# Two cross-attention layers: key stacks loaded a unit ahead in layer 0, slot by slot in layer 1

## The reference

```
layer 0:  q = x Wq + 2 x Aq Bq          32 heads
          k, v likewise from ctx          8 heads, each shared by 4 query heads
          x = x + (softmax(q k' / 4) v) Wo'    (Wo' with its low-rank part)
layer 1:  q = x Wq + bq, k = ctx Wk + bk, v = ctx Wv + bv    32 heads each
          masked keys get -inf before the softmax
          x = layernorm(x + (softmax(q k' / 4) v) Wo + bo) * g + b
```

## Time and profile before

| | |
|---|---|
| median of the runs | 1661.51 us (1660.65 to 1664.09) |
| the profiled execution's own time | 1668.17 us |
| its span, first to last instruction | 1666.3 us |
| mean granted TensorE clock | 0.967 of 2.4 GHz |
| PE, VectorE, ScalarE, GpSimd busy | 95%, 73%, 60%, 11% of the span |
| DMA | 168.22 MB, 101 GB/s over the span |

### The profile page before, as it was taken

One profiled execution on the slowest core, in us unless ns is written; L12 is line 12 of the kernel. 1 busy time (PEld: TensorE's weight loads), 2 busy tenths in 40 slices (PEclk: granted clock), 3 DMA queues, 4 the chain that ended last, 5 costly groups with the idle time before them and its releaser, 6 DMA issues.

```text
span 1666.3 us, 42831 instructions
## 1 busy us (share of the span) xinstructions
PE 1581.1 (95%) x17828; PEld 1133.7 (68%) x17828; DVE 1216.4 (73%) x2669; ACT 1005.8 (60%) x1855; POOL 177.6 (11%) x274
## 2 busy tenths in 40 slices
PE   6899999999999999899989999999989999999997
PEld 3657666676666765655667777776767677777763
DVE  2667778677777777678867777588777778778782
ACT  0146666566666666576656666656656666666665
POOL 2000221001221011121211110000000001000000
PEclk8789999999999999999999999999999999999998
DMA  8645542534454233455436455634375346644520
GB/s 218 140 130 143 123 109 81 145 75 93 103 141 122 63 78 84 82 118 138 101 81 124 89 94 90 156 58 81 71 149 85 65 69 123 128 76 71 85 40 14
DMA packets 93970, 168.22 MB, mean 101 GB/s; under 512 B 21900, under 2 KB 70060, under 8 KB 93776
## 3 DMA queue, kind: packets, MB, share of 16 engines
q1 hardware_dynamic: 93776, 165.48, 47.1%
HBM read 114.62 MB, written 48.78 MB: 98 GB/s over the span
## 4 chain that ended last, share of the span: by engine, by line
PE 87%; issue 5%; DMA 2%; DVE 2%; SPq 1%; ACT 1%; POOL 0%; DVEq 0%; POOLq 0%
PE value L1093 23%; PE ring L1057 14%; PE work L1001 13%; PE work L1021 13%; PE score L1070 9%; PE score L1075 7%; PE work L1046 4%; PE work L1115 3%; DVE chunk_max L1240 1%; PE work L1029 1%; DMA m_dram<-m_turned 1%; ACT p_sb L1154 1%; PE work L984 1%; DMA ctx_sb<-ctxT 0%; SPq L1431 0%
## 5 line engine op out<-in xcount | busy, mean ns | idle before, releaser
L1240 DVE TENSOR_REDUCE chunk_max<-ring 128x1 f32<-128x402 f32 x2048 | 1046.0, 567 | 314.1 <-PE ring L1057 304.7
L1154 ACT ACTIVATE p_sb<-score 124x512 f32<-124x512 f32 (+1 forms) x1664 | 929.8, 597 | 546.7 <-PE score L1070 278.8
L1057 PE MATMUL ring<-k_stack,q_stack 64*128 64x402 f32 x2048 | 728.7, 448 | 42.4 <-issue 32.9
L1057 PEld LDWEIGHTS ring<-k_stack,q_stack 64*128 64x128 f32 x2048 | 339.9, 189 | 143.4 <-issue 64.1
L1093 PE MATMUL value<-p_sb,v_sb 124*32 124x256 f32 x6656 | 432.1, 388 | 1.6 <-issue 0.8
L1070 PE MATMUL score<-q_stack,k_stack 64*124 64x512 f32 (+1 forms) x832 | 365.4, 506 | 5.1 <-ACT p_sb L1154 3.3
L1075 PE MATMUL score<-q_stack,k_stack 64*124 64x256 f32 (+1 forms) x1664 | 344.2, 315 | 4.1 <-ACT p_sb L1154 2.0
L1021 PE MATMUL work<-wv,ctx_sb 64*124 64x128 f32 x3840 | 333.4, 276 | 4.8 <-issue 4.7
L1021 PEld LDWEIGHTS work<-wv,ctx_sb 64*124 64x124 f32 x3840 | 317.8, 187 | 9.0 <-issue 6.2
L1001 PE MATMUL work<-ctx_sb,wk 64*128 64x402 f32 x1280 | 295.7, 507 | 2.2 <-ACT full L1165 1.0
L1093 PEld LDWEIGHTS value<-p_sb,v_sb 124*32 124x32 f32 x6656 | 184.5, 110 | 161.0 <-issue 51.9
(11 more groups left out here) (64 smaller groups left out, 365.7 us busy)
## 6 DMA issues: line engine op xcount, KB each, us to landing
k_stack<-k_dram SPq DMA_DIRECT2D x288, 200.1 KB
k_dram<-k_parts SPq DMA_DIRECT2D x60, 402.0 KB, 3.2
ctx_sb<-ctxT SPq DMA_DIRECT2D x24, 992.0 KB, 12.2
q_stack<-q_dram SPq DMA_DIRECT2D x64, 256.0 KB, 3.7
q_dram<-q_parts SPq DMA_DIRECT2D x96, 128.0 KB
k_dram<-k_parts SPq DMA_DIRECT2D x20, 395.0 KB, 3.3
wq<-l_Wq SPq DMA_DIRECT2D x2, 1024.0 KB, 7.4
xt_sb<-xT SPq DMA_DIRECT2D x4, 512.0 KB, 11.6
```

The lines of the kernel that those rows point to most:

```text
L1057: engine.matmul(ring[bank_of["max", u, half, m]][:, 0:MW], q_stack[rows, u % 3, j, q * P:(q + 1) * P], k_stack[rows, 2 * (z % 3) + (u % 2 ...
L1154: engine.activation(p_sb[0:tn, n % PLACES, :], score_bank[n % 2][0:tn, :], ACT.Exp, scale=SCALE).then_inc(s_exp, 1)
L1240: engine.tensor_reduce(chunk_max[:, u % 2, half, m // NM, m % NM:m % NM + 1], ring[bank_of["max", u, half, m]][:, 0:MW], AX.X, ALU.max)\
```

## The change

It has five parts. Layer 0's stacks are ordered a unit sooner (at unit 0 for unit 2, then at odd units u for u + 3), with key products due a unit (13 tiles) and most query products 7 tiles sooner. Layer 1's stacks come in twelve loads of one slot each, first the six of slot 0, which count on a semaphore of their own (`s_slot`), then the six of slot 1. The mask rows are loaded only for the first three units of a batch entry, one for each place, and ahead of the keys. A maximum of slot 0 waits for `s_slot` alone, one of slot 1 and every score for both. Pending writes are emitted when due, each by itself, "write q" after 3 tiles instead of 1, and are flushed by kind. The planner's times for stacks change to match.

```diff
     def step(self, *name):
-        if name[0] == "stack":
-            self.write_keys(None)
         self.steps.append(name)
 
-    def write_keys(self, now):
-
-        while self.writes and (now is None or self.writes[0][0] <= now):
-            self.steps.append(self.writes.pop(0)[1])
+    def write_keys(self, now, *kinds):
+
+        due = [x for x in self.writes if (x[0] <= now if now is not None else x[1][0] in kinds)]
+        for x in due:
+            self.writes.remove(x)
+            self.steps.append(x[1])
...
         if kind == "k":
-            self.write_keys(None)
+            self.write_keys(None, "write k")
...
-            self.writes.append((self.now + 1, ("write q", name[1])))
+            self.writes.append((self.now + 3, ("write q", name[1])))
...
+    def slot_at(self, unit, m):
+
+        return (self.first_slot if m < self.CHUNKS // 4 else self.stack_at)[unit]
...
-        self.enter("half", half, max(self.ring_free[bank], self.stack_at[unit], self.query_at[unit]))
+        self.enter("half", half, max(self.ring_free[bank], self.slot_at(unit, m), self.query_at[unit]))
...
-            if self.next_stack == unit + 2:
+            if self.next_stack is not None and unit == self.at_unit:
                 self.load_stack()
...
-    LOAD_CTX, LOAD_STACK, LOAD_QUERY, LOAD_ROWS = 5500, 9000, 3000, 6500
+    LOAD_CTX, LOAD_STACK, LOAD_SLOT, LOAD_QUERY, LOAD_ROWS = 5500, 11000, 6000, 3000, 6500
...
-            todo += [(start + (UB - 2) * NT - 5, start + 2, ("k", b, g)) for g in k]
+            todo += [(start + (UB - 3) * NT - 5, start + 2, ("k", b, g)) for g in k]
...
         for pair in range(2, UNITS // 2):
-            todo.append(((2 * pair - 2) * NT - 6, (2 * pair - 3) * NT - 6, ("q", pair)))
+            due = (2 * pair - 2) * NT - (6 if pair >= L0 // 2 and pair % 4 == 0 else NT)
+            todo.append((due, due - NT, ("q", pair)))
...
         if u + 2 < self.UNITS:
-            for g in range(self.NM // 2):
-                self.ensure("k", self.seq_of(u + 2), g)
             self.ensure("q", (u + 2) // 2)
-            self.write_keys(None)
+            if ("write q", (u + 2) // 2) in [x[1] for x in self.writes]:
+                self.write_keys(None, "write q")
             self.load_queries(u + 2)
-            self.next_stack = u + 2
-            if u in self.rows_at:
-                self.load_stack()
+            self.next_stack = u + 2 if u + 2 >= L0 or u == 0 else u + 3 if u % 2 and u + 3 < L0 else None
+            if self.next_stack is not None:
+                seq = self.seq_of(self.next_stack)
+                for g in range(self.NM // 2):
+                    self.ensure("k", seq, g)
+                if seq in [x[1][1] for x in self.writes if x[1][0] == "write k"]:
+                    self.write_keys(None, "write k")
+                if u in self.rows_at:
+                    self.load_stack()
...
-        if u >= self.L0 or u % 2 == 0:
-            self.arrival = max(self.arrival, max(self.free) + 2000) + self.LOAD_STACK
-        self.stack_at[u] = self.arrival
-        self.stacked, self.next_stack = u, None
+        both = max(self.arrival, max(self.free) + 2000)
+        self.arrival = both + (self.LOAD_STACK if u < self.L0 else 2 * self.LOAD_SLOT)
+        self.first_slot[u] = both + self.LOAD_SLOT if u >= self.L0 else self.arrival
+        self.stack_at[u], self.stacked, self.next_stack = self.arrival, u, None
+        if u < self.L0:
+            self.stack_at[u + 1], self.first_slot[u + 1], self.stacked = self.arrival, self.arrival, u + 1
         self.load_ctx()
...
+    def mask_changes(z):
+        return z >= L0 // 2 and (z - L0 // 2) % UB < 3
...
-            total[z % 3] += 6 + 2 * (z >= L0 // 2)
+            total[z % 3] += 6
+            slots[z % 3] += (6 + 2 * mask_changes(z)) * (z >= L0 // 2)
             kst_loads.append(16 * total[z % 3])
+            slot_loads.append(16 * slots[z % 3])
...
-        def stack_ready(e, z):
-            e.wait_ge(s_kst[z % 3], kst_loads[z])
+        def stack_ready(e, z, j=1):
+            if z >= L0 // 2:
+                e.wait_ge(s_slot[z % 3], slot_loads[z])
+            if z < L0 // 2 or j:
+                e.wait_ge(s_kst[z % 3], kst_loads[z])
             e.wait_ge(s_kx[z % 3], 32)
...
-                    if u < L0 and u % 2:
-                        continue
...
-                    if u >= L0:
+                    if mask_changes(z):
                         b = (u - L0) // UB
                         e.wait_ge(s_mask, 1)
...
-                                             .broadcast_to([1, 2, T])).then_inc(s_kst[g], 16)
+                                             .broadcast_to([1, 2, T])).then_inc(s_slot[g], 16)
+                    if u < L0:
+                        for r, part in KPARTS:
+                            keys = raw(k_dram[seq, part, row:row + count, :])
+                            for half in range(2):
+                                at = 64 * half + HD * r
+                                engine.dma_start(raw(k_stack[at:at + HD, 2 * g:2 * g + 2, :]),
+                                                 keys.rearrange("(j d) t -> d j t", j=2)).then_inc(s_kst[g], 16)
+                    else:
+                        for j in range(2):
+                            for r, part in KPARTS:
+                                keys = raw(k_dram[seq, part, row + 2 * HD * j:row + 2 * HD * (j + 1), :])
+                                for half in range(2):
+                                    at = 64 * half + HD * r
+                                    engine.dma_start(raw(k_stack[at:at + HD, 2 * g + j, :]),
+                                                     keys.rearrange("(e d) t -> e d t", e=2)[half])\
+                                        .then_inc(s_kst[g] if j else s_slot[g], 16)
```

More of the change, by code:

```diff
@@ L75, in __init__ @@
         self.ctx_now, self.ctx_since, self.chunk_product = [0] * NC, [0] * NC, [None] * NC
-        self.rows_at, self.stack_at, self.arrival = {}, {0: 0.0, 1: 0.0}, 0.0
+        self.rows_at, self.stack_at, self.first_slot, self.arrival = {}, {0: 0.0, 1: 0.0}, {0: 0.0, 1: 0.0}, 0.0
         self.query_at, self.finished_units = {}, 0
@@ L364, in prologue @@
         self.step("read mask")
-        self.write_keys(None)
+        self.write_keys(None, "write k", "write q")
         self.load_queries(0)
@@ L608, in state @@
             self.bank, self.before, self.made, self.taken, self.swaps, self.number, self.ctx_after,
-            self.split_number, self.key_number, self.count, self.exp_end, self.rows_at, self.stack_at, self.query_at, self.first)]
+            self.split_number, self.key_number, self.count, self.exp_end, self.rows_at, self.stack_at, self.first_slot, self.query_at, self.first)]
         users = [x.copy() for x in self.ctx_users]
@@ L622, in go_back @@
         (self.bank, self.before, self.made, self.taken, self.swaps, self.number, self.ctx_after,
-         self.split_number, self.key_number, self.count, self.exp_end, self.rows_at, self.stack_at, self.query_at,
-         self.first) = \
+         self.split_number, self.key_number, self.count, self.exp_end, self.rows_at, self.stack_at, self.first_slot,
+         self.query_at, self.first) = \
             [x.copy() for x in tables]
@@ L676, in advance @@
                 max(0.0, max(self.ring_free[self.ring_turn % len(self.ring_owner)],
-                             self.stack_at[self.max_at[row] // (CHUNKS // 2)],
+                             self.slot_at(*divmod(self.max_at[row], CHUNKS // 2)),
                              self.query_at[self.max_at[row] // (CHUNKS // 2)]) - self.begins("half", row))
@@ L904, in cross_attention_pair @@
         s_kst = [sem(f"s_kst{i}") for i in range(3)]
+        s_slot = [sem(f"s_slot{i}") for i in range(3)]
         s_kx = [sem(f"s_kx{i}") for i in range(3)]
@@ L1054, in tensor @@
                     bank_free(e, ("max", u, half, m))
-                    stack_ready(e, z)
+                    stack_ready(e, z, j)
                     queries_ready(e, u)
@@ L1538, in sync @@
                         e.wait_ge(s_kx[g], 32)
-                    for r, part in KPARTS:
-                        keys = raw(k_dram[seq, part, row:row + count, :])
-                        for half in range(2):
-                            own = keys.rearrange("(j d) t -> d j t", j=2) if u < L0 else \
-                                keys.rearrange("(j e d) t -> e d j t", j=2, e=2)[half]
-                            at = 64 * half + HD * r
-                            engine.dma_start(raw(k_stack[at:at + HD, 2 * g:2 * g + 2, :]), own).then_inc(s_kst[g], 16)
-                    if u >= L0:
+                    if mask_changes(z):
                         b = (u - L0) // UB
```

4 lines of the change are left out of this document (2 added, 2 removed).

## The result

The changed kernel takes 1655.70 us, the median of 14 runs (1648.08 to 1662.97), against 1665.02 us for the kernel before in 14 runs that include the three shown (1659.11 to 1670.45). The ratio is 0.9938, with a 95% interval of 0.9919 to 0.9956: 10 us faster, where 42 were forecast, and 8 us above the range's upper end of 1648. The profiled execution took 1657.94 us.

A forecast was written before the change was run, and what follows sets the result against it. PE was taken as the bound, losing 50.2 us to key-stack waits and their half clock. Terms 28.2 + 22.0 + 1 - 3 - 6 = 42 us off the 1661.51 us median gave 1620 us, range 1604 to 1648.

The forecast's parts named there:

- What bounds the kernel: PE, 95% busy: eleven waits for key stacks, 32.8 us, plus 17.35 us lost at half clock, 50.2 us in all.
- Layer 0's stacks a unit ahead: Units 8 to 26: six stack waits go, 18.3 us, with 9.9 us of clock; 28.2 us gained.
- Layer 1: First slot usable sooner: waits of unit 33 and four more go, 14.5 us plus 7.5 of clock; 22.0 us gained.
- rival (3): Small loads cost by their number, so each stack's second slot comes late: about 1935 us, milder form 1730; chance 0.04.
- Writes no longer in one line: SyncE's queue: maxima writes no longer held behind key writes; gain between 0 and 3 us, taken as 1.
- New waits: Whole kernel's order drawn anew: 6 us allowed for waits that turn up elsewhere, 0 to 25 at the ends.
- rival (2): Waits come back elsewhere, at context chunks, maxima rows or exponentials one step behind: 1650 to 1664 us; chance 0.10.
- SyncE's extra issue: 192 loads added, 40 mask rows dropped: context chunks behind layer 1's stacks issue later, a loss of 3 us.
- The signs that the prediction named: If right: no "issue" maxima waits in layer 0, clock above 0.975, PE above 96%; if wrong, same idle under other lines.

The follow-up runs named there:

- all_three_ahead: Changed kernel, SyncE's queue alone: unit 0's maxima ahead of unit 2's stack and context, unit 41's maxima load earlier, layer 1's early loads later; 1620.31 us.
- twelve_loads_everywhere: Kernel before with all 48 stacks, both layers, in twelve loads of one slot, no other change; 1621.19 us, ratio 0.9735.
- slots_alone: Kernel before with layer 1's part alone: twelve loads, slot 0's maxima waiting for six, fewer mask rows, order redrawn under the old write rule; 1640.85 us.
- twelve_loads_one_wait: Kernel before, order untouched, layer 1's stacks in twelve loads of one slot, all maxima still waiting for all of them; 1640.95 us, ratio 0.9868.
- old_write_rule: Changed kernel with the old rule for writes: in order, flushed by a stack step and at a unit's entry; 1629.16 us, ratio 0.9786.
- m0_ahead: Changed kernel with unit 0's maxima write and load ahead of unit 2's stack and four context chunks in SyncE's queue; 1639.36 us, ratio 0.9847.
- context_behind_maxima: Changed kernel with all_three_ahead's moves, plus two context chunks each loaded behind the maxima's rows of units 28 and 39; 1619.25 us, ratio 0.9735.

## Why the prediction was wrong

**What bounds the kernel: right.** PE with eleven waits for key stacks, paid twice through the clock. Two ways of taking them away, all_three_ahead and twelve_loads_everywhere, give 42 and 44 us of the 50 I had counted; they differ in layer 0 and share the form of the loads in layer 1.

**Layer 0's stacks a unit ahead, 28.2 us: right in its mechanism, and within 4 us.** The six waits are gone in the changed profile, units 8 to 31 are 30 us shorter, and the part alone is worth 24 us once its surroundings are cleared. That figure holds unit 33's wait as well, which I had counted to layer 1, so some of the agreement is luck.

**Layer 1, 22.0 us: the size right, the mechanism wrong.** I credited it to the first slot's earlier release. slots_alone and twelve_loads_one_wait have the same ratio, 0.9868, and only one of them has that release; with intervals of 0.003 on either side, a few us of it could still hide there. What gained was the rate, and my step that has the second slot "at 12.5 us as before" took the rate of six loads for that of twelve. That the size came out is luck in part: the value products' waits, 4.7 us, went too, and the term didn't have them.

**The size of the loads.** The windows show twelve loads of 100 KB faster than six of 200 KB. The Trainium skill (DMA: Bandwidth & Descriptors, Rules for kernel authors) says to coalesce many small transfers into one large one; here the measurement decides against it, and rival (3), which was built on that rule, fell.

**The step that failed** is "Writes no longer in one line", priced at "Gain between 0 and 3 us; I take 1". It measured as a loss of 25 us (old_write_rule), which is most of the 32 us between the 42 forecast and the 10 measured. I had read the removed flush only as something that holds maxima up behind key writes. It was also what put them ahead of the stack and the context. The prediction's list of what is queued on SyncE looked at what stands behind the stack in layer 1 (the maxima's write 14 us later, past a key write at 890.32 that the earlier trace rows leaves out) and never walked the queue at unit 0, where a stack, four context chunks and the maxima become due within 12 us. The row that showed it, the first score's neighbourhood in SyncE's queue, was there to be asked for.

**New waits, 6 us at a range of 0 to 25:** the mean was too low. Units 5, 28 and 39 have such waits (13.2 us in the changed kernel), and those of units 5 and 41 cost 17 to 19 us, the step from m0_ahead to all_three_ahead, clock and all. Unit 41's belongs to the term above, since the old rule for writes takes it away; the other three stand under either rule and are this term's own. All are of one kind, a small transfer behind a large one in SyncE's queue, and rival (2), at 0.10, described it: "context chunks, maxima rows and exponentials are each one step behind". Its price was about right and its chance too small. The range's end should have taken in the loss of what a removed flush orders.

**SyncE's extra issue, 3 us:** not seen as a cost anywhere. twelve_loads_everywhere has 288 more loads than the kernel before and is 44 us faster.

**The signs that the prediction named.** The maxima's waits with "issue" went, as for a right forecast. The mean clock was 0.965 instead of above 0.975, PE was busy for 95% instead of above 96%, and nearly the same idle time stood under other lines, the sign for rival (2).

**Readings that were off and changed nothing.** The cut at 107 us isn't the first score, which stands at 77.4. The windows of 1 us while unit 26's stack moves range from 103 to 145 GB/s from 683 to 692 us, not from 115 to 141, after two of 299 and 230.

## What to carry to other kernels

When a rule that orders a queue is removed, walk the queue at the places where most falls due together, above all at the start; a small transfer on which PE depends must be issued before megabytes on which nothing depends yet. Before a load is hidden by restructuring, try its shape: in layer 0, one row for each partition and load was worth 20 us and a unit of lead with its surroundings cleared 24, and the first is a handful of lines. In layer 1, where no lead was to be had, it was worth 22. And run the reverse edit: the same order put into the kernel before gave the wait and 23.6 us in one run, without the rest of the change.

## What the runs showed of the hardware

- The shape of a load sets its rate. Loads of 16 partitions with one row of 6.4 KB each moved at 163 to 164 GB/s; with two rows of 6.4 KB, or two of 3.2 KB, at 128 to 141, in the windows of one stack each. Over the whole kernel the packets took 65 us less of the DMA engines' time for the same 165.5 MB.
- A DMA of 16 KB behind 4.4 MB waits for it: issued at 82.56, its reader released at 94.41, where 2.5 us do with a free queue. The Trainium skill (DMA: Bandwidth & Descriptors, Queues, rings and completion order) says that each DMA engine takes the descriptors of a ring in order; the trace agrees. The issue itself also stalled, 4.67 us for one DMA against 0.50.
- The granted clock can fall without a long wait. In context_behind_maxima it is 0.50 for 13.65 us from 742.05, after waits of at most 0.9 us. In the changed kernel's profile it is 0.50 for 10.24 us from 1512.22, where the longest wait near by is 0.65 us, before a score that waited for ScalarE. all_three_ahead has the same wait in the same place, 0.66 us before the score at 1480.31, and its clock didn't fall there. PE is busy for all of the 10.24 us (the windows above), so 5 us are lost. Such falls may be part of why the changed kernel's runs spread over 15 us; that wasn't tested.
